# The router computed with one batch per partition, and the first tile's second half normalised and rounded behind the choice of experts

## The chip, the cores and the metric

One core of a Trainium2 chip. The metric is the device time of one execution in microseconds (us). TensorE (PE in the profile, PEld its weight loads) does the matmuls, VectorE is DVE, ScalarE is ACT, GpSimd is POOL, SyncE (SP) issues most of the transfers. Each engine runs its own queue in order; where one needs another's result, its instruction waits for a semaphore. SBUF is the memory on the chip, PSUM the banks that TensorE writes.

## The reference, cut to what matters

x is (8, 64, 32, 32): 8 batches, 64 channels, 1024 tokens. First comes a channel attention block with a residual, then a mixture of experts whose router sees only the mean token of a batch, so each batch has one choice of two experts out of eight:

```python
x = x + _L0_conv_ref(_ln_c(x), Wqkv, bqkv, Wout, bout, 8)
t = _to_tokens(x)
t = t + _L0_ffn_ref(_ln_t(t), Wr, br, W1, b1, W2, b2, gamma, beta)
# in _L0_ffn_ref, x being _ln_t(t):
logits = jnp.mean(x, axis=1) @ Wr + br                       # (8 batches, 8 experts)
routing_weights = jax.nn.softmax(logits, axis=-1)
expected_loads = routing_weights.sum(axis=0) * (N / B)
scale = jnp.where(expected_loads > capacity, capacity / expected_loads, 1.0)
routing_weights = jax.nn.softmax(routing_weights * scale, axis=-1)
top_w, top_i = jax.lax.top_k(rw_tok, K)                      # K = 2
top_w = jax.nn.softmax(top_w, axis=-1)
h = jax.nn.gelu(jnp.einsum('nd,edf->enf', xf, W1) + b1[:, None, :], approximate=False)
y = jnp.einsum('enf,efd->end', h, W2) + b2[:, None, :]
out = _layer_norm(out + x, gamma, beta)                      # out: the two chosen y, weighted
```

The kernel computes only the two chosen experts of each batch.

## The kernel before, in words

The data lie with channels on the partitions, two batches to a tile of 128 partitions: four tiles p = 0 to 3, each with 1024 columns. After the attention block `T` holds the residual stream, 128 x 1024 per tile; columns 0 to 511 of a tile are its batch half b = 0, 512 to 1023 its half b = 1. The queues of all engines are written out by hand, and nothing reorders them.

Around the change this happens. `scores(p)` multiplies T by the router's weights on TensorE, `evac_scores` copies the result to SBUF, `turn_scores` transposes it into `ps_sc`. `turned_stats` and `rstd2` give `r2`, one over the deviation of every token (semaphore `pow2`). `weigh_scores` and `sum_scores` (DVE) weigh the scores with r2 and sum them; `logits` sums over the partitions with a matrix of ones, which leaves all 64 logits on each of the 128 partitions. From there DVE and ACT work through softmax, loads, scale, `largest` (the eight largest values of a batch, `m8`) and `indices` (their places, `i8`). The semaphore `top` tells that indices are there, batches 0 and 1 first. The second softmax and the weights of the two experts are worked out with two Tanh on ACT; `wk` holds the weights.

Meanwhile the tile's values are normalised: `spread2(p, b)` spreads r2 over the channels with matmuls into the PSUM bank `rb[p][b]`, `normal2(p, b)` (DVE) multiplies T by it into `UF` (semaphores s_uf0 to s_uf7), `round_hi` (ACT) rounds that to fp16 in `HI`, and `low` (POOL) puts the rest in `LO`. For p = 1 and 3 spread2 works with bf16 rows in `RR` (made by split3 on POOL, turn2 on PE and a copy on ACT); for p = 0 and 2 with fp32 matmuls from r2 itself. `centre_w1` and `centre_w2` centre the experts' weights; `split_w1` (ACT) and `low_w1` (POOL) split W1 into two fp16 parts in `w1hl`; `w2c` is centred W2.

Once the experts are known, `gather_w1` copies the weights of one batch's expert into `w1g` and `gather_w2` those of W2 times `wk` into `w2g`. The expert layers are steps: `up(step, i)` is the first matmul of an expert for one batch (six matmuls of 512 columns: HI with both weight parts, LO with one), `gelu(step, i)` on ACT, and `down(step, i)` the second matmul into `y_ps` (bank pC). `residual3(p, ...)` puts the centred input into y_ps ahead of the down matmuls, from `ST`, a copy of HI and LO that SP's transfers make. y_ps and the two halves of rb[2] are the same bank, so residual3(0, (0,)) waits until normal2(2, 0) has read rb[2][0] (s_uf4), and residual3(0, (1,)) until normal2(2, 1) has (s_uf5).

PE's queue runs on as up(0,0), up(0,1), up(1,0), residual3(0,(0,)), down(0,0), up(1,1), residual3(0,(1,)), down(0,1), down(1,0), down(1,1), up(2,0). Gelu needs another table of functions on ACT than Exp, so the kernel calls a one-column Gelu (`gtab`) ahead of the first real one.

Of the kernel before, what the change touches and what calls it, by code (L numbers as in the profile page):

```python
# [8 lines left out]
BF16 = mybir.dt.bfloat16  # L9
# [43 lines left out]
def build_program(nc, x_tok, x_cha, small, w12, consts, constb, out):  # L53
# [11 lines left out]
    with ExitStack() as ctx:  # L65
# [23 lines left out]
        w1f = SQ[:, 0, :]  # L89
# [40 lines left out]
        brz = sb("brz", [P, B * E])  # L130
        ssw = sb("ssw", [P, B * E])
        ones_m = sb("ones_m", [P, P])
        rout = sb("rout", [P, 4, B * E])
        rx = sb("rx", [P, 2, (E + 1) * B])
        rsm = sb("rsm", [P, 8, B])
        m8 = sb("m8", [P, B, 8])
        i8 = sb("i8", [P, B, 8], U32)
        wk = sb("wk", [P, B, TOP])
# [3 lines left out]
        i8f = sb("i8f", [P, TOP, B])  # L142
        hot = sb("hot", [P, TOP, B * E])
# [49 lines left out]
        rb = [[pB[:, HALF:N], pA[:, HALF:N]], [pS[:, :], pM[:, :]], [pC[:, 0:HALF], pC[:, HALF:N]], [pS[:, :], pM[:, :]]]  # L193
# [4 lines left out]
        def pair_view(ap):  # L198
# [19 lines left out]
        ps_lg = pM[:, 0:B * E]  # L218
        px = [pB[:, i * B * E:(i + 1) * B * E] for i in range(3)]
# [46 lines left out]
        def _(sp):  # L266
# [12 lines left out]
            for b in range(2):  # L279
                cols = slice(b * HALF, (b + 1) * HALF)  # L280
                for half, src, done in ((0, HI, s["hi"]), (1, LO, s["lo"])):
                    sp.wait_ge(done, b + 1)
                    for h in range(2):
                        sp.dma_start(ST[half * C:(half + 1) * C, b, h * HALF:(h + 1) * HALF],
                                     src[h * C:(h + 1) * C, 0, cols]).then_inc(s_st[b], 16)
            for p in range(1, NP):
                for half, src, done in ((0, HI, s["hi"]), (1, LO, s["lo"])):
                    if (p, half) == (NP - 1, 0):
                        sp.wait_ge(s["hi3"], 2)
                    else:  # L290
                        sp.wait_ge(done, 2 * p + 2 - half)
# [24 lines left out]
        def _(act):  # L316
# [32 lines left out]
            def split_w1(h):  # L349
# [4 lines left out]
                nc.scalar.mul(w1hl[:, e, 0, :], src, S_W).then_inc(s["w1h"], 1)  # L354
                nc.scalar.mul(w1f[:, h * HALF:(h + 1) * HALF], ps_w1[h], S_W).then_inc(s["w1f"], 1)
# [80 lines left out]
            act.wait_ge(s["top"], 1)  # L436
            first = {(0, 0): nc.scalar.value_load(i8[0:1, 0, 0:1], min_val=0, max_val=E - 1)}
            act.wait_ge(s["w1h"], 2)
            act.wait_ge(s["w1l"], 2)
            nc.scalar.copy(w1g[:, 0, 0, 0, :, :], w1hl[:, bass.ds(first[0, 0], 1), :, :]).then_inc(s["w1g_first"], 1)  # L440
            act.wait_ge(s["rx2"], 1)
            nc.scalar.activation(rx[:, 1, :], rx[:, 0, :], ACT.Tanh, scale=0.5).then_inc(s["rexp2"], 1)

            def half_tanh():
                act.wait_ge(s["rx3"], 1)
                nc.scalar.activation(rsm[:, 7, :], rsm[:, 6, :], ACT.Tanh, scale=0.5).then_inc(s["half_tanh"], 1)
# [56 lines left out]
            half_tanh()  # L503
# [39 lines left out]
        def _(pool):  # L543
# [36 lines left out]
            def load_experts(p):  # L580
                pool.wait_ge(s["top"], min(p + 1, 3))
                experts = [[load_expert(p, k, b) for b in range(2)] for k in range(TOP)]
# [26 lines left out]
            nc.gpsimd.memset(ones_m[:, :], 1.0 / (S_U * N)).then_inc(s["onesm"], 1)  # L609
# [4 lines left out]
            for h in range(2):  # L614
# [15 lines left out]
            split3(nc.gpsimd, link, 0, 2, r2[:, 1:NP:2, :], s["s2"])  # L630
            low_w1(0)
            low_w1(1)
            low(0, 0)
            low(0, 1)
            pool.wait_ge(s["top"], 1)
            pool.wait_ge(s["w1h"], 2)
            pool.wait_ge(s["w1l"], 2)
            pool.wait_ge(s["w2v"], 2)
            experts = [[0, 0], [0, 0]]
            for k, b in ((0, 1), (1, 0), (1, 1)):  # L640
                experts[k][b] = load_expert(0, k, b)
                gather_w1(0, k, b, experts[k][b])
            experts[0][0] = load_expert(0, 0, 0)
# [28 lines left out]
        def _(dve):  # L672
# [107 lines left out]
            def weigh_scores(g):  # L780

                dve.wait_ge(s["sc"], 2 * g + 2)
                dve.wait_ge(s["pow2"], 1)
                src = ps_sc[g][:, 0:4 * P].rearrange("p (j r) -> p j r", r=32)[:, :, 0:2 * E]
                link(nc.vector.tensor_tensor(
                    sw[:, 2 * g * P:2 * (g + 1) * P].rearrange("p (j h e) -> p j h e", h=2, e=E),
                    src.rearrange("p j (h e) -> p j h e", h=2),
                    r2[:, 2 * g:2 * g + 2, :].rearrange("p n (j h) -> p (n j) h", h=2).unsqueeze(3)
                    .broadcast_to([P, 2 * CH, 2, E]), ALU.mult))
# [736 lines left out]
```

## Time and profile before

| what | us |
|---|---|
| runs shown: median, lowest, highest of 3 | 94.47, 94.15, 95.64 |
| the profiled execution | 94.27 |
| its span, first to last instruction | 92.4 |
| PE busy | 81.0 (88%) |
| DVE busy | 62.1 |
| ACT busy | 51.0 |
| POOL busy | 38.7 |

The span is 1.87 us shorter than the time of the same execution; that rest lies around the span. The mean granted TensorE clock over the span is 0.991 of full speed. Rows of the profile give a start and a duration in us, the engine, the line of the kernel, the operation, what it writes and reads, and in brackets how long its engine was idle before it and what released it.

### The profile page before, as it was taken

The numbers are of one execution on the slowest core, as the hardware profiler recorded it, in microseconds if no ns is written. First come the engines' busy times: TensorE is split into PE (matmuls) and PEld (weight loads), VectorE is DVE, ScalarE is ACT, GpSimd is POOL, SyncE is SP. The second block draws the span as 40 slices with busy tenths as digits, with TensorE's granted clock in tenths as the row PEclk, the third lists the DMA queues.
The fourth block names the chain that finished last, engine by engine and source line by source line (L and its number), as shares of the span: only waits on it lengthen the run. The fifth ranks groups of instructions, "written<-read, shape, count | busy, mean of one in ns | idle before, by whom it ended". The sixth has DMA issues, their size and how long they took to land.

```text
span 92.4 us, 2203 instructions
## 1 busy us (share of the span) xinstructions
PE 81.0 (88%) x723; PEld 42.8 (46%) x723; DVE 62.1 (67%) x225; ACT 51.0 (55%) x91; POOL 38.7 (42%) x90
## 2 busy tenths in 40 slices
PE   4995999999799999997769996999989999998900
PEld 1343699899654356486623341323324332344500
DVE  0089998981749798899899869741555374649560
ACT  0050505416388533379759989967995879644000
POOL 6000090000000050299334499947960850499900
PEclk9999999999999999999999999999999999999996
DMA  2899999991000000001430033880050036008573
GB/s 42 260 401 321 296 269 249 264 257 30 0 7 0 0 0 0 11 0 30 112 86 4 7 83 75 198 200 16 0 121 0 0 86 141 0 19 200 141 202 127
DMA packets 6715, 9.82 MB, mean 106 GB/s; under 512 B 1073, under 2 KB 3633, under 8 KB 6705
## 3 DMA queue, kind: packets, MB, share of 16 engines
q1 hardware_dynamic: 5408, 7.56, 32.1%
q10 hardware_dynamic: 1296, 2.13, 7.6%
q8 instruction: 6, 0.10, 0.4%
q14 instruction: 5, 0.03, 0.1%
HBM read 5.49 MB, written 2.10 MB: 82 GB/s over the span
## 4 chain that ended last, share of the span: by engine, by line
PE 52%; DVE 12%; ACT 12%; DMA 8%; POOL 7%; issue 4%; ACTq 2%; DVEq 0%; POOLq 0%
PE pC L1351 10%; DMA cst<-consts_dram 8%; PE pA L1327 5%; ACT H L480 5%; PE pB L1033 4%; PE pS L1033 4%; PE pA L1043 4%; POOL r L603 4%; PE pB L1327 3%; POOL XT L252 3%; PE pC L1095 2%; PE pS L1095 2%; PE pC L1343 2%; PE pA L1110 2%; DVE bst L762 2%
## 5 line engine op out<-in xcount | busy, mean ns | idle before, releaser
L1351 PE MATMUL pC<-H,w2g 128*64 128x512 f32 x64 | 15.9, 603 | 0.0
L705 DVE BATCH_NORM_STATS2 bst<-XT 128x6 f32<-128x128 f32 x32 | 6.5, 286 | 5.0 <-DMA XT<-x_tok_dram 5.0
L627 POOL TENSOR_TENSOR T<-UF,X 128x512 f32<-128x512 f32 x1 | 1.3, 1270 | 19.0 <-ACT UF L417 19.0
L1246 PE MATMUL pM<-wz 128*128 128x512 bf16 x25 | 7.7, 473 | 1.3 <-POOL wz L552 1.3
L480 ACT ACTIVATE H<-pA,b1s 128x1024 f32<-128x1024 f32 x6 | 6.7, 1115 | 2.8 <-PE pA L1327 2.7
L562 POOL TENSOR_TENSOR LO<-UF,HI 128x512 f16<-128x512 f32 x7 | 8.0, 1158 | 0.0
L578 POOL COPY w1g<-w1hl 128x256 f16 x15 | 5.9, 425 | 3.8 <-issue 2.5
L480 ACT ACTIVATE H<-pB,b1s 128x1024 f32<-128x1024 f32 x6 | 6.7, 1123 | 0.1
L242 POOL CAST R<-r 128x16 bf16<-128x16 f32 (+1 forms) x4 | 0.8, 201 | 14.2 <-DVE r L696 14.2
L1327 PE MATMUL pA<-HI,w1g 64*128 64x512 f16 x32 | 4.9, 380 | 2.1 <-ACT H L480 1.5
L252 POOL TENSOR_TENSOR XT<-XT,T 128x512 f32<-128x512 f32 x5 | 6.3, 1271 | 0.0
L1351 PEld LDWEIGHTS pC<-H,w2g 128*64 128x64 f32 x64 | 4.0, 136 | 5.0 <-issue 4.1
L332 ACT COPY U<-pA 128x1024 f32<-128x1024 f32 x4 | 4.0, 1012 | 3.8 <-PE pA L1043 3.7
L259 POOL TENSOR_TENSOR UT<-XT,rt 128x512 f32<-128x512 f32 x2 | 2.0, 1045 | 9.1 <-DVE UT L259 9.1
L949 DVE TENSOR_SCALAR U<-pC,c,wsm 128x512 f32<-128x512 f32 x6 | 4.7, 800 | 1.2 <-PE pC L1351 0.9
L594 POOL TENSOR_TENSOR w2g<-w2c,wk 128x64 f32<-128x64 f32 x16 | 4.7, 319 | 1.6 <-DVE wk L894 1.4
L1246 PEld LDWEIGHTS pM<-wz 128*128 128x128 bf16 x25 | 2.7, 117 | 5.3 <-issue 2.7
L1327 PE MATMUL pB<-HI,w1g 64*128 64x512 f16 x32 | 4.9, 378 | 0.0
L382 ACT ACTIVATE T<-T,wsm 128x1024 f32<-128x1024 f32 x4 | 4.6, 1158 | 0.0
L493 ACT ACTIVATE SQ<-pC,c 128x512 f32<-128x512 f32 x6 | 4.0, 688 | 1.1 <-DVE U L949 0.6
L968 DVE COPY RR<-pS 48x128 bf16<-48x128 bf16 x3 | 0.6, 216 | 5.8 <-PE pS L1163 5.8
L385 ACT ACT_TABLE_LOAD x1 | 1.3, 1283 | 5.6 <-issue 5.6
(247 smaller groups left out, 196.4 us busy)
## 6 DMA issues: line engine op xcount, KB each, us to landing
X<-x_cha_dram SPq DMA_DIRECT2D x16, 128.0 KB, 10.1
out_dram<-XT SPq DMA_DIRECT2D x11, 128.0 KB, 2.4
XT<-x_tok_dram SPq DMA_DIRECT2D x2, 512.0 KB, 9.2
ST<-HI SPq DMA_DIRECT2D x6, 128.0 KB, 2.4
ST<-LO SPq DMA_DIRECT2D x6, 128.0 KB, 2.4
XT<-x_tok_dram SPq DMA_DIRECT2D x2, 256.0 KB, 4.7
XT<-x_tok_dram ACTq DMA_DIRECT2D x2, 256.0 KB, 4.9
w_sb<-w_dram ACTq DMA_DIRECT2D x4, 128.0 KB, 8.9
```

The costliest lines, as they stand in the source:

```text
L252: engine.tensor_tensor(OUT[:, p, cols], V[:, p, cols], T[:, p, cols], ALU.add).then_inc(s_fin[2 * p + h], 1)
L382: nc.scalar.activation(T[:, p, :], T[:, p, :], ACT.Identity, bias=w("beta")).then_inc(s["tbeta"], 1)
L480: nc.scalar.activation(H[:, step % 2, i, :], h_ps[i][:, :], ACT.Gelu, bias=bias, scale=1.0 / (S_U * S_W)).then_inc(s["gelu"], 1)
L562: nc.gpsimd.tensor_tensor(LO[:, p, cols], UF[:, p, cols], HI[:, p, cols], ALU.subtract).then_inc(s["lo"], 1)
L578: nc.gpsimd.tensor_copy(w1g[:, p % 2, k, b, :, :], w1hl[:, bass.ds(expert, 1), :, :]).then_inc(s["w1g"], 1)
L594: nc.gpsimd.tensor_tensor(w2g[:, p % 2, b, k, :], w2c[:, bass.ds(experts[k][b] * C, C)], wk[:, 2 * p + b, k:k + 1].broadcast_to([P, C]), A ...
L705: return nc.vector.bn_stats(bst[:, p, j, :], XT[:, p, j * P:(j + 1) * P].rearrange("p (b c) -> p c b", b=2))
L949: nc.vector.tensor_scalar(ZS[:, p, cols], y_ps[:, cols], c2[:, i:i + 1], w("gamma"), ALU.add, ALU.mult).then_inc(s["zs"], 1)
L1033: last = mm(ps_g[g][:, l * G1:(l + 1) * G1], UT[:, p, j, 1:P + 1], UT[:, p, j, :], start=(j == 0), stop=(j == CH - 1))
L1246: mm(pM[:, :], wz[:, 0:P], wz[:, :], start=True, stop=True)
L1327: last = mm(h_ps[i][:, h * HALF:(h + 1) * HALF], w1g[h * C:(h + 1) * C, p % 2, k, b, a, :], src[h * C:(h + 1) * C, p, b * HALF:(b + 1) * H ...
L1351: last = mm(half(y_ps[:, b * HALF:(b + 1) * HALF], h), w2g[:, p % 2, b, k, :], H[:, step % 2, i, h * HALF:(h + 1) * HALF], start=False, st ...
```

## The change: what it does

The router is computed with one batch on each of eight partitions. The raw scores are copied to SBUF (`copy_scores`, ACT), `sum_scores` on TensorE multiplies them by r2 and sums over the tokens (eight matmuls of 8 rows and 64 columns), and two small DVE operations and one matmul (`logits`) give an 8 x 8 tile of logits. Exp on ACT gives the sums as well (accum_out). `loads` is a matmul over the eight partitions. One MAX and one MAX_INDEX serve all batches, so `top` comes once. The second softmax uses Exp instead of Tanh (`ex2`, `e01`, `eu`), and one matmul (`choice`) brings weights and indices from 8 partitions to all 128 (`ps_bc`, copied to `wk`).

Of the first tile, normal2(0, 1) now stands behind MAX_INDEX on DVE, and round_hi(0, 1) behind the wait for `top` on ACT; LO of that half is made on DVE (semaphore `lo01`) instead of POOL. The copies of `w2c` move from ACT to DVE, half of LO of W1 moves from POOL to DVE, and the first expert's gather from ACT to POOL. spread2(2, *) works with RR rows instead of fp32; spread2(1, *) moves behind up(0, 1). normal2 runs in the order (1,0), (2,0), (1,1), (2,1).

```diff
         def normal2(p, b):
                 i = 2 * p + b
-                dve.wait_ge(s["rb"], i + 1)
+                dve.wait_ge(s["rb"], 2 * (0, 2, 1, 3)[p] + b + 1)
...
-            weigh_scores(0)
-            weigh_scores(1)
-            for g in range(2):
-                last = sum_scores(g)
-            last.then_inc(s["ssw"], 1)
+            dve.wait_ge(s["w1h"], 1)
+            nc.vector.tensor_tensor(w1hl[:, 0:E // 2, 1, :], ps_w1[0].rearrange("p (e f) -> p e f", f=F),
+                                    w1hl[:, 0:E // 2, 0, :], ALU.subtract).then_inc(s["w1l0"], 1)
+            dve.wait_ge(s["lq"], 1)
...
             normal2(0, 0)
+            dve.wait_ge(s["lg"], 1)
+            nc.vector.tensor_reduce(nlm[:, :], ps_lg, AX_X, ALU.max, negate=True).then_inc(s["nlm"], 1)
+            dve.wait_ge(s["rexp1"], 1)
+            nc.vector.reciprocal(ri[:, :], es[:, :]).then_inc(s["ri"], 1)
+            dve.wait_ge(s["load"], 1)
...
+            nc.vector.max(m8[:, :], rout[:, :]).then_inc(s["m8"], 1)
+            dve.wait_ge(s["m8"], 1)
+            nc.vector.max_index(i8[:, :], m8[:, :], rout[:, :]).then_inc(s["top"], 1)
+            normal2(0, 1)
+            dve.wait_ge(s["rexp2"], 2)
...
+            for h in range(2):
+                nc.vector.tensor_copy(w2c[:, h * HALF // 2:(h + 1) * HALF // 2], ps_w2[h]).then_inc(s["w2v"], 1)
...
+            dve.wait_ge(s["hi"], 2)
+            nc.vector.tensor_tensor(LO[:, 0, HALF:N], UF[:, 0, HALF:N], HI[:, 0, HALF:N],
+                                    ALU.subtract).then_inc(s["lo01"], 1)
+            dve.wait_ge(s["bc"], 1)
+            nc.vector.tensor_copy(wk[:, :, :], ps_bc.rearrange("p (b k) -> p b k", b=B)).then_inc(s["wkd"], 1)
+            normal2(1, 0)
+            normal2(2, 0)
+            normal2(1, 1)
+            normal2(2, 1)
...
             round_hi(0, 0)
-            act.wait_ge(s["rx1"], 1)
-            nc.scalar.activation(px[0], rout[:, 1, :], ACT.Exp).then_inc(s["rexp1"], 1)
             act.wait_ge(s["rt2"], 1)
-            nc.scalar.copy(RR[:, :, :], ps_rt2.rearrange("p (k n) -> p k n", k=2)).then_inc(s["rr2"], 1)
+            nc.scalar.copy(RR[:, :, :], ps_rt2.rearrange("p (k n) -> p k n", k=3)).then_inc(s["rr2"], 1)
+            act.wait_ge(s["rout"], 1)
+            nc.scalar.activation(ex2[:, :], rout[:, :], ACT.Exp, accum_out=es2[:, :]).then_inc(s["rexp2"], 1)
...
+            act.wait_ge(s["top"], 1)
             round_hi(0, 1)
-            act.wait_ge(s["w2p"], 1)
-            for h in range(2):
-                nc.scalar.copy(w2c[:, h * HALF // 2:(h + 1) * HALF // 2], ps_w2[h]).then_inc(s["w2v"], 1)
...
+            act.wait_ge(s["de"], 1)
+            nc.scalar.activation(eu[:, :], de[:, :], ACT.Exp, scale=ri2[:, :]).then_inc(s["rexp3"], 1)
             nc.scalar.activation(gtab[:, :], w("bout"), ACT.Gelu)
...
+            centre_w1()
             turn_scores(2)
             turn_scores(3)
-            centre_w1()
-            bias_logits()
+            sum_scores()
             spread2(0, 0)
+            logits()
             spread2(0, 1)
-            logits()
             turn2()
+            loads()
             for i in range(2):
                 centre_w2(i)
             for b in range(2):
-                spread2(1, b)
-            for b in range(2):
                 spread2(2, b)
...
+            up(0, 0)
+            choice()
+            up(0, 1)
             for b in range(2):
-                up(0, b)
+                spread2(1, b)
             up(1, 0)
```

On PE, from the spreading for the third tile (rb[2], bank pC) to the second step's first up, before:

```order
L1201 MATMUL pC<-cst,r2 64x128 [waits s_w2v,s_pow2]
L1201 MATMUL pC<-cst,r2 64x128 x7
L1201 MATMUL pC<-cst,r2 64x128 [waits s_w2v,s_pow2]
L1201 MATMUL pC<-cst,r2 64x128 x7
L1327 MATMUL pA<-HI,w1g 128x512 [waits s_w1g_first,s_hi,s_w1l,s_w1h]
L1327 MATMUL pA<-HI,w1g 128x512 x3
L1327 MATMUL pA<-LO,w1g 128x512 [waits s_lo]
L1327 MATMUL pA<-LO,w1g 128x512
L1327 MATMUL pB<-HI,w1g 128x512 [waits s_hi,s_w1g]
L1327 MATMUL pB<-HI,w1g 128x512 x3
```

and now (L1153 is spread2 from RR, L1214 `choice`, L1326 `up`):

```order
L1153 MATMUL pC<-RR,cstb 128x128 [waits s_w2v,s_rr2,s_pow2]
L1153 MATMUL pC<-RR,cstb 128x128 x3
L1153 MATMUL pC<-RR,cstb 128x128 [waits s_w2v,s_rr2,s_pow2]
L1153 MATMUL pC<-RR,cstb 128x128 x3
L1326 MATMUL pA<-HI,w1g 128x512 [waits s_hi,s_w1g,s_w1f]
L1326 MATMUL pA<-HI,w1g 128x512 x3
L1326 MATMUL pA<-LO,w1g 128x512 [waits s_lo]
L1326 MATMUL pA<-LO,w1g 128x512
L1214 MATMUL pM<-mk,ones 128x32 [waits s_mk,s_ones8]
L1326 MATMUL pB<-HI,w1g 128x512 [waits s_hi,s_w1g]
L1326 MATMUL pB<-HI,w1g 128x512 x3
L1326 MATMUL pB<-LO,w1g 128x512 [waits s_lo01]
```

The sixteen fp32 matmuls for the third tile have become eight bf16 ones that wait for RR too, choice stands between the first two ups with a wait for mk, and the second up takes its LO half behind lo01. Behind that second up:

```order
L1326 MATMUL pB<-LO,w1g 128x512
L1153 MATMUL pS<-RR,cstb 128x128 [waits s_bc,s_rr2,s_pow2]
L1153 MATMUL pS<-RR,cstb 128x128 x3
L1153 MATMUL pM<-RR,cstb 128x128 [waits s_wkd,s_rr2,s_pow2]
L1153 MATMUL pM<-RR,cstb 128x128 x3
L1326 MATMUL pA<-HI,w1g 128x512 [waits s_gelu,s_w1g]
L1326 MATMUL pA<-HI,w1g 128x512 x3
L1326 MATMUL pA<-LO,w1g 128x512 x2
L1342 MATMUL pC<-ST,cstb 64x512 [waits s_st0,s_uf4]
```

The spreading for the second tile (pS, pM) has moved here, its first half behind bc and its second behind wkd, ahead of the second step's up and of residual3 (L1342), which waits for s_uf4.

On DVE, from the largest values to the weights, before:

```order
L863 MAX m8<-rout 128x8 [waits s_dve]
L863 MAX m8<-rout 128x8 x3
L866 MAX_INDEX i8<-m8,rout 128x8 [waits s_dve]
L866 MAX_INDEX i8<-m8,rout 128x8
L863 MAX m8<-rout 128x8 x4
L876 TENSOR_TENSOR rx<-m8 128x8 [waits s_dve]
L877 TENSOR_TENSOR rx<-rout,m8 128x64
L800 TENSOR_TENSOR UF<-T,pC 128x512 [waits s_rb]
L883 TENSOR_SCALAR rx<-rx 128x72 [waits s_rexp2]
L884 RECIPROCAL rx<-rx 128x72 [waits s_dve]
L885 TENSOR_REDUCE rsm<-rx 128x8 [waits s_dve]
L886 TENSOR_SCALAR rsm<-rsm 128x8 [waits s_dve]
```

and now, to the copy of wk and the first two normal2 behind it (left out are four small operations on 8 partitions, of which the first after the wait for eu is dn):

```order
L799 TENSOR_TENSOR UF<-T,pB 128x512 [waits s_rb]
L859 RECIPROCAL ri2<-es2 8x1 [waits s_rexp2]
L860 TENSOR_TENSOR de<-e01 8x1
L863 COPY w2c<-pC 128x256 [waits s_w2p]
L863 COPY w2c<-pC 128x256
...
L870 TENSOR_TENSOR mk<-val,s8 8x32 [waits s_dve]
L873 TENSOR_TENSOR LO<-UF,HI 128x512 [waits s_hi]
L876 COPY wk<-pM 128x32 [waits s_bc]
L799 TENSOR_TENSOR UF<-T,pS 128x512 [waits s_rb]
L799 TENSOR_TENSOR UF<-T,pC 128x512 [waits s_rb]
```

The half of the first tile (UF<-T,pB), the w2c copies and LO have come between the choice and the third tile's normal2 (UF<-T,pC), which before stood directly behind the MAX instructions.

On ACT, from the Exp of the router to the first Gelu, before:

```order
L427 ACTIVATE pB<-rout 128x64 [waits s_rx1]
L429 COPY RR<-pA 48x256 [waits s_rt2]
L378 CAST HI<-UF 128x512 [waits s_uf1]
L433 COPY w2c<-pC 128x256 [waits s_w2p]
L433 COPY w2c<-pC 128x256
L435 ACT_TABLE_LOAD
L435 ACTIVATE gtab<-wsm 128x1
L437 TENSOR_LOAD i8 [waits s_top]
L437 ISA x2
L440 ISA [waits s_w1l,s_w1h]
L440 COPY w1g<-w1hl 128x256
L442 ACTIVATE rx<-rx 128x72 [waits s_rx2]
```

and now:

```order
L455 ACTIVATE ex2,es2<-rout 8x8 [waits s_rout]
L457 ACTIVATE e01<-m8 8x2 [waits s_m8]
L399 CAST HI<-UF 128x512 [waits s_uf1,s_top]
L460 TENSOR_LOAD i8
L460 ISA x2
L462 ACTIVATE eu<-de,ri2 8x1 [waits s_de]
L463 ACT_TABLE_LOAD
L463 ACTIVATE gtab<-wsm 128x1
L497 ISA [waits s_mm1]
L497 ACTIVATE H<-pA,wsm 128x1024
```

The second rounding has moved behind `top`, and the table load behind it and behind the Exp that makes eu; the copies of w2c and the first gather have left ACT.

## Rows read from the trace of the kernel before

**Rows 1.** The chain that ended last, 38 to 52 us: start, duration, what.

```profile
38.39 0.24 DVE r L696
...
39.64 1.15 DVE ssw L792 x2
...
43.61 1.28 ACT L435
...
45.63 0.41 ACT w1g L440
...
46.34 0.84 PE pA L1327 x6
...
47.30 1.12 ACT H L480
...
48.56 0.82 PE pA L1327 x6
...
49.39 0.34 PE pC L1343 x2
...
51.34 0.34 PE pC L1343 x2
```

**Rows 2.** PE in order of time: start, duration, line, operation.

```profile
37.51 0.69 PE L1227 MATMUL pC<-w_sb,cst 64*128 64x512 f32 x1
...
38.93 1.09 PE L1201 MATMUL pB<-cst,r 128*64 128x128 f32 x16
...
40.84 0.43 PE L1213 MATMUL pM<-ssw,ones_m 128*128 128x64 f32 x2
...
42.56 0.38 PE L1168 MATMUL pS<-RR,cstb 48*128 48x128 bf16 x4
...
42.79 0.38 PE L1168 MATMUL pM<-RR,cstb 48*128 48x128 bf16 x4
```

**Rows 3.** ACT in order of time, 20 to 45 us.

```profile
20.47 0.35 ACT L337 ACTIVATE Ex<-sm,nmx 128x64 f32<-128x64 f32 x1 [2.96 <-DVE nmx L736]
...
20.72 0.19 ACT L337 ACTIVATION_READ_ACCUMULATOR Ex<-sm,nmx 128x1 f32 x1
...
38.67 0.60 ACT L354 ACTIVATE w1hl<-pC 128x512 f16<-128x512 f32 x1 [1.58 <-PE pA L1227]
...
42.43 0.62 ACT L378 CAST HI<-UF 128x512 f16<-128x512 f32 x1
...
42.95 0.64 ACT L433 COPY w2c<-pC 128x256 f32<-128x256 f32 x2
...
44.90 0.20 ACT L435 ACTIVATE gtab<-wsm 128x1 f32<-128x1 f32 x1
```

**Rows 4.** ACT line that reads the expert number, from its queue.

```profile
L437 ACTq TENSOR_LOAD <-i x1: 480/480/480, 44.7 to 44.7; - x1
```

**Rows 5.** DVE in order of time, 38 to 54 us.

```profile
38.72 0.42 DVE L785 TENSOR_TENSOR sw<-pS,r 128x256 f32<-128x256 f32 x1
...
41.72 0.68 DVE L800 TENSOR_TENSOR UF<-T,pA 128x512 f32<-128x512 f32 x1
...
43.33 0.21 DVE L858 RECIPROCAL pB<-rsm 128x8 f32<-128x8 f32 x1
...
44.52 0.16 DVE L866 FIND_INDEX8 i<-m,rout 128x8 uint32<-128x8 f32 x1
...
53.28 0.22 DVE L928 TENSOR_REDUCE c<-hb 128x8 f32<-128x64 f32 x1
```

**Rows 6.** POOL in order of time.

```profile
42.11 2.27 POOL L562 TENSOR_TENSOR LO<-UF,HI 128x512 f16<-128x512 f32 x2
...
45.63 0.40 POOL L578 COPY w1g<-w1hl 128x256 f16 x1 [1.25 <-DVE i L866]
```

**Rows 7.** DMA issues by line: KB each, us from issue to landing.

```profile
ST<-LO SPq DMA_DIRECT2D x4, 64.0 KB, 2.1
```

**Rows 8.** Stretch after the last matmul: busy of PE, PEld, DVE, ACT, POOL; then PEclk.

```profile
87.90:90.50 2.60, 0.00 (x0) 0.00 (x0) 1.25 (x4) 0.00 (x0) 0.04 (x1) 1.00 0.75 213
```

More of the change, by code:

```diff
@@ L129, in build_program @@
         SR = sb("SR", [P, 2, 2 * P])
[L130 to L138, printed above, removed]
+        cendS = sb("cendS", [P, P])
+        ones = sb("ones", [B, P])
+        s8 = sb("s8", [P, B])
+        lm = sb("lm", [P, B + 1, E])
+        ls = sb("ls", [P, E])
+        nlm = sb("nlm", [B, 1])
+        ex = sb("ex", [B, E])
+        es = sb("es", [B, 1])
+        ri = sb("ri", [B, 1])
+        fe = sb("fe", [B, 2, E])
+        rout = sb("rout", [B, E])
+        ex2 = sb("ex2", [B, E])
+        es2 = sb("es2", [B, 1])
+        ri2 = sb("ri2", [B, 1])
+        m8 = sb("m8", [B, 8])
+        i8 = sb("i8", [B, 8], U32)
+        e01 = sb("e01", [B, TOP])
+        de = sb("de", [B, 1])
+        eu = sb("eu", [B, 1])
+        dn = sb("dn", [B, 1])
+        val = sb("val", [B, 2 * TOP])
+        mk = sb("mk", [B, B, 2 * TOP])
+        wk = sb("wk", [P, B, 2 * TOP])
         w1g = sb("w1g", [P, 2, TOP, 2, 2, F], F16)
@@ L280, in _ @@
                 cols = slice(b * HALF, (b + 1) * HALF)
-                for half, src, done in ((0, HI, s["hi"]), (1, LO, s["lo"])):
-                    sp.wait_ge(done, b + 1)
+                for half, src, done in ((0, HI, s["hi"]), (1, LO, s["lo"] if b == 0 else s["lo01"])):
+                    sp.wait_ge(done, 1 if half else b + 1)
                     for h in range(2):
@@ L290, in _ @@
                     else:
-                        sp.wait_ge(done, 2 * p + 2 - half)
+                        sp.wait_ge(done, 2 * p if half else 2 * p + 2)
                     if half:
@@ L437, in _ @@
[L437 to L446, printed above, removed]
@@ L502, in _ @@
             gelu(0, 0)
-            half_tanh()
             gelu(0, 1)
@@ L580, in load_experts @@
             def load_experts(p):
[L581 to L582 removed]
+                experts = [[0, 0] for k in range(TOP)]
+                if p:
+                    experts = [[load_expert(p, k, b) for b in range(2)] for k in range(TOP)]
                 for k in range(TOP):
                     for b in range(2):
+                        if p == 0:
+                            experts[k][b] = load_expert(p, k, b)
                         gather_w1(p, k, b, experts[k][b])
@@ L894, in _ @@
-            nc.vector.tensor_scalar(wk[:, :, 1], rsm[:, 7, :], 0.5, 0.5, ALU.mult, ALU.add).then_inc(s["wkd"], 1)
-            indices(2)
-            indices(3).then_inc(s["top"], 1)
-            for b in range(2):
-                normal2(1, b)
-            for i in range(4, B):
-                last = indices(i)
-            last.then_inc(s["top"], 1)
-            dve.wait_ge(s["top"], 3)
             dve.wait_ge(s["iota"], E)
+            dve.wait_ge(s["wkd"], 1)
+            dve.wait_ge(s_uf[2], 1)
@@ L1174, in turn2 @@
                 pe.wait_ge(s["s2"], 1)
-                pe.wait_ge(s["w1f"], 2)
-                for i in range(2):
+                pe.wait_ge(s["scs"], 2)
+                for i in range(NP - 1):
                     last = turn(ps_rt2[:, i * P:(i + 1) * P], i)
@@ L1324, in up @@
                     elif k == 0 and n != 1:
-                        pe.wait_ge(done, 2 * p + b + 1 - (n == 2 and p >= 2))
+                        pe.wait_ge(done, 2 * p + b + 1 - ((p >= 1) + (p >= 2) if n == 2 else 0))
                     for h in range(2):
```

226 lines of the change are left out of this document (107 added, 119 removed).

## The prediction

> **What bounds the kernel now.** I read the chain that ended last first, because the change lies in one short stretch and only what it does to that chain counts. From the last step of r2 on DVE at 38.39 the chain runs through the summing of the scores, then through ACT (rounding, copies of w2c, the load of the Gelu table at 43.61), the first expert's gather at 45.63, the first up at 46.34, the first Gelu at 47.30, and from 48.56 on it stays on PE: up, residual3 at 49.39, down, up, residual3 at 51.34 [rows 1]. In the order of time I then read PE, ACT, DVE and POOL of that stretch for the durations [rows 2, 3, 5, 6]. The reader is to see two marks: the first Gelu starts at 47.30, and residual3(0,(0,)) at 49.39. Behind that PE has no gap in the chain until after 51.34, so the end moves by as much as residual3 moves, unless something later is late. I found nothing later that becomes earlier or later by itself: all ups, Gelus and downs stay.
>
> **The change: the router, up to `top`.** r2 is there at 38.39 + 0.24 = 38.63, as before [rows 1]. What follows it changes.
> - The centring of W1 moves ahead of the last two turned scores. It started at 37.51 and ACT took its result at 38.67 [rows 2, 3]. The two blocks change places, so the pair ends where it ended, at 38.65 at the latest; as the transposes then wait for ACT no longer, I take 38.4. The turned scores thus come 0.9 later than the 37.5 of before, nearly hidden by the r2 chain, which needs until 38.63.
> - ACT copies the second half of the scores (128 x 256, some 0.4 us, by the DVE row of that size at 0.42 [rows 5] and the 0.64 of two ACT copies of it [rows 3]): 38.85. Eight matmuls of 64 columns give lq. The trace has none with 8 rows; it lies between 0.43, a single fp32 product of 64 columns, and 1.09, eight of 128 columns [rows 2]. I take 0.55, nearer to the first since four of them write different strips of rows: 39.45.
> - In exchange the two weighing and two summing steps go, which ran from 38.72 to 39.64 + 1.15 = 40.79 [rows 1, 5]. Two small DVE steps at about 0.22 follow; ls is there at 39.95. The new subtraction of W1 on DVE (38.7 to 39.4, by the 0.68 of a 512-column row [rows 5]) lies under the wait for lq.
> - PE spreads the first half (1.09 [rows 2]) from 39.4 to 40.45, DVE normalises it until 41.15, logits is done by then, and the maximum at 41.35.
> - Exp with its sum: an Exp of 64 columns and the reading of its sum end 0.44 after the start (20.47 to 20.72 + 0.19 [rows 3]); here 41.8. Reciprocal (0.21 [rows 5]) 42.05. The matmul `loads` at 0.43 [rows 2] 42.5. Three small steps, MAX and MAX_INDEX at 0.2 to 0.25 each: `top` at 43.65.
>
> Before, `top` was at 44.52 + 0.16 = 44.68 [rows 5]. So the choice comes 1.0 us earlier. The uncertain terms are lq (0.43 to 1.09, that is -0.1 to +0.5) and seven handovers between engines, which I took at 0.05 (summing ends at 40.79, PE's next weight-carrying matmul starts at 40.84 [rows 1, 2]) and which could cost 0.1 more each: +0.7.
>
> **What eats this gain.** Before, DVE had the half normal2(0,1) behind it at 41.72, beside the Exp [rows 5]. Now it stands behind `top`:
> - DVE: normal2(0,1) 43.7 to 44.35; ri2 and de to 44.7; the two w2c copies, 0.64 on ACT [rows 3] and up to twice 0.42 on DVE [rows 5], I take 0.75: 45.45.
> - PE: spread2(2,*) waits for w2v, because its bank is that of w2c, and it stands ahead of up(0,0). It is now eight bf16 matmuls, which the other tile's took from 42.53 to 42.79 + 0.38 = 43.17, 0.64 [rows 2]: 45.5 to 46.1. So PE waits for w2v, while POOL has the first gather ready: it came 0.95 after `top` and takes 0.40 [rows 5, 6], thus by 45.05. up(0,0) at 0.84 [rows 1] ends at 46.95.
> - ACT: rounding of that half (0.62 [rows 3]) 44.4 to 45.0; the expert number is read meanwhile (0.48 [rows 4]); eu to 45.3; the table load at 1.28 [rows 1] to 46.6; gtab at 0.20 [rows 3] to 46.8. The first Gelu then waits for PE only, and starts at 47.05. It gains 0.25 against 47.30, not 1.0. The cover over the table load is thin: 0.15.
> - The weights: mk on DVE from eu by four small steps to 46.3, LO of the half to 47.0, PE takes choice at 46.95, up(0,1) to 47.9 and spread2(1,0) to 48.2 (half of the 0.64). wk is copied at 47.3, and POOL's first gather of W2 is in time for the down.
> - DVE: normal2(1,0) 48.25 to 48.95, normal2(2,0) to 49.65, each 0.68 [rows 5]. Only then may residual3(0,(0,)) write its bank: 49.7 against 49.39 [rows 1]. Before, that half was normalised directly behind MAX and nobody waited for it. up(1,0), from 48.4 to 49.25, is no longer the last thing that residual3 waits for.
>
> **The sum:** residual3 moves by 49.7 - 49.39 = +0.3 us. Behind it, residual3(0,(1,)) waits for normal2(2,1), at 49.65 + 2 x 0.68 = 51.05, and for the transfer of LO, whose issue is at 47.1 plus a second one of about 1.2 and 2.1 to land [rows 7], near 50.4; both are ahead of 51.34 + 0.3. The biases' block on DVE ended at 53.28 + 0.22 [rows 5]; it starts 0.2 later than before and ends near 53.7, still ahead of the second tile's evacuation. On POOL, low of the half (half of 2.27 [rows 6]) is gone and gathers are earlier, which frees about 1 us that no one waits for. The profiled execution took 94.27, so I predict 94.27 + 0.3 = 94.6, which is 0.1 over the median of the runs shown, 94.47.
>
> The Trainium skill ("ScalarE: Activation LUTs", section "What ACT_TABLE_LOAD costs") adds a drain of about 1.38 us to the 1.28 of a table load for every change of set. Here the load starts right behind the w2c copies and gtab follows it at 44.90, 1.29 after 43.61 [rows 1, 3], so the trace shows no drain there. By the page the first Gelu would come 1.38 later than I reckon by way of the table.
>
> **The rivals.**
> - *Faster: the waits for w2v and s_uf4 are shorter.* If lq and the w2c copies take their lower ends and PE hands over faster, 0.3 + 0.1 + 0.1 go, and with shorter small steps (8 partitions instead of 128) some 0.3 more. Then residual3 could come at 48.9, but up(1,0) bounds it: Gelu at 46.9 at the earliest gives up(1,0) to 49.0. Gain 0.4: 93.9. For it speaks that the choice is 1 us earlier; against it, that a DVE step of 8 columns costs 0.16 to 0.21 [rows 5] by its start alone.
> - *Slower: the longer hand-to-hand chain.* The router now crosses between engines some ten times up to the weights. With lq at 1.09 and the handovers 0.1 us dearer, everything behind the r2 step is 1.1 later, and since residual3 is at the end of that same chain, nothing absorbs it: 94.6 + 0.9 = 95.5. It decides for slower than before from the point at which `top` comes after 43.35, by the sum above.
> - *The table load is not hidden.* It now stands behind an Exp of eight rows instead of a copy; if that made it cost its row once more, 1.28 [rows 1], the first Gelu would be at 48.1, up(1,0) would run from 49.3 to 50.2 instead of ending at 49.39, and the time would be 94.27 + 0.8 = 95.1. That gtab followed the load at once [rows 3] speaks against it. The page named above would make it much the same.
> - *The clock.* PE has nothing from the centring of W2 (about 43.4) to 45.5, a pause of 2.1 us. The only pause of that length that the trace shows is after the last matmul: in 2.6 us the granted clock stayed at 1.00 (2.4 GHz) [rows 8]. If it fell to 1.2 GHz all the same, the next ups would take twice 0.84 each, and two of them give +1.7: 96.3.
>
> **How the numbers follow.** Forecast 94.6 with chance 0.5; faster rival 93.9 with 0.2; longer chain 95.5 with 0.2; table 0.05; clock 0.05. The range holds 0.8: it leaves out the clock and the outer halves of the two large rivals, 93.6 to 95.7. A measurement of this kernel can tell about 2%, 1.9 us; no case but the clock's comes near that. Chances: faster 0.05, same 0.86, slower 0.09.
>
> **What would show it.** In the trace of the changed kernel: MAX_INDEX ending near 43.65; the w2c copies on DVE near 45.45 and spread2(2,*) right behind them; the table load from 45.3 to 46.6; the first Gelu near 47.05; residual3 held by UF<-T,pC of DVE and starting near 49.7; the granted clock at 1.00 throughout. The prediction is wrong in its core if residual3 is held by up(1,0) or the Gelu instead, or if a step before 38.6 moves.

## The result and the profile after

The changed kernel is slower: 97.78 us in the median of 5 executions (96.83 to 98.13) against 94.48 (94.15 to 95.64), a ratio of 1.0323 with a 95% interval of 1.0272 to 1.0374. The profiled execution took 96.83 with a span of 94.5; before, it was 94.27 with 92.4. So 2.1 of its 2.56 us lie in the span and 0.46 outside it. Outside the span lay 1.87 in the profiled execution of before, 1.8 to 2.2 in its other executions and 2.3 in all five of the changed kernel; that part stays unexplained.

The first look is at the clock, since the forecast stood on a full one. The view of stretches of the changed kernel (start and end; length; busy time of PE, PEld, DVE, ACT, POOL, each with its number of instructions; then the granted clock):

```profile
43.20:45.60 2.40, 0.01 (x1) 0.00 (x0) 2.27 (x11) 1.03 (x5) 0.58 (x2) 1.00 0.43 107
45.60:47.40 1.80, 1.65 (x18) 1.11 (x20) 1.39 (x5) 1.77 (x4) 0.92 (x3) 1.00 0.25 63
47.40:50.60 3.20, 3.20 (x20) 1.56 (x20) 1.69 (x5) 2.11 (x2) 1.43 (x6) 0.51 0.21 51
50.60:52.00 1.40, 1.40 (x9) 0.40 (x10) 1.37 (x6) 1.07 (x2) 1.36 (x4) 0.90 0.00 0
```

PE has nothing to do for 2.4 us, works again from 45.6, and at 47.4 the clock falls from 2.4 to 1.2 GHz and stays there for 3.4 us, until 50.8, through nothing but matmuls. The other four executions have only a mean clock, and it is lower still: 0.949 to 0.954, against 0.968 in the profiled one and 0.991 in the profiled one of before. (A mean also holds the end of the program, where the clock falls in every kept trace although PE has no more work, and where that costs nothing.) So the profiled execution, the fastest of the five, is the mildest case. As an estimate from the means, if the end was as in the profiled one (2.7 us at half clock), the others ran 6 to 7 us of matmuls at 1.2 GHz, as experiments 2 and 10 show it in a trace.

The chain of the changed kernel, where it answers to [rows 1]:

```profile
42.12 0.21 DVE fe L849
...
42.35 1.07 DVE fe L850
...
43.89 0.23 DVE i L856 x2
44.11 0.58 DVE UF L799
...
44.83 0.68 DVE w2c L863 x2
...
45.64 0.49 PE pC L1153 x6
...
47.01 0.37 PE pM L1214 x2
47.38 1.28 PE pB L1326 x6
48.66 0.42 PE pS L1153 x4
49.08 0.21 PE pM L1153 x2
...
49.51 1.28 PE pA L1326 x5
50.79 0.40 PE pC L1342 x2
```

Up to 47.38 the reader can lay this beside the forecast's own times: w2c copied at 45.5 (forecast 45.45), spread2(2,*) from 45.6, choice at 47.0 (46.95). From there each up takes 1.28 us instead of the 0.82 to 0.84 of [rows 1], and residual3 comes at 50.79 instead of 49.39, right behind up(1,0). One step stands out before that: L850, an operation on 8 x 8 elements, took 1.07 us. Beside it ran this on POOL (order of time, changed kernel):

```profile
42.24 1.15 POOL L578 TENSOR_TENSOR LO<-UF,HI 128x512 f16<-128x512 f32 x1 [1.05 <-ACT HI L399]
```

POOL's subtraction ended at 43.39, the small step at 43.41. The same happens once more behind the first layer (order of time, changed kernel, POOL and DVE):

```profile
55.15 2.27 POOL L578 TENSOR_TENSOR LO<-UF,HI 128x512 f16<-128x512 f32 x2 [0.36 <-ACT HI L399]
...
56.56 1.41 DVE L920 TENSOR_TENSOR LO<-UF,HI 128x512 f16<-128x512 f32 x1
```

A step of this shape takes 0.67 alone. PE's first moment rows, at 57.93 before, are at 60.03 here: the 1.4 us from residual3 have become 2.1, which is the whole difference of the spans.

### The profile page after: what moved, and what is told of

Its sections match the earlier page's. It is cut to its first block, busy times and chain, and to the rows that moved or that the text cites. A ratio compares the mean times of both kernels' runs of the same rounds, so it can differ in the third digit from the quotient of the medians.

```text
span 94.5 us, 2174 instructions
## 1 busy us (share of the span) xinstructions
PE 81.5 (86%) x718; PEld 42.7 (45%) x718; DVE 60.5 (64%) x200; ACT 51.1 (54%) x93; POOL 37.7 (40%) x93
## 4 chain that ended last, share of the span: by engine, by line
PE 56%; DVE 14%; DMA 8%; POOL 7%; ACT 7%; issue 3%; ACTq 1%; DVEq 0%; POOLq 0%
PE pC L1350 10%; DMA cst<-consts_dram 8%; PE pB L1018 4%; PE pA L1028 4%; PE pA L1326 4%; PE pS L1018 4%; POOL r L620 4%; PE pB L1326 4%; ACT H L497 3%; DVE UF L799 3%; POOL XT L264 3%; DVE U L936 2%; PE pA L1095 2%; PE pC L1080 2%; PE pC L1342 2%
## 5 line engine op out<-in xcount | busy, mean ns | idle before, releaser
L1248 PE MATMUL pM<-wz 128*128 128x512 bf16 x25 | 8.3, 503 | 1.3 <-POOL wz L568 1.3
L578 POOL TENSOR_TENSOR LO<-UF,HI 128x512 f16<-128x512 f32 x6 | 6.9, 1158 | 2.1 <-ACT HI L399 2.1
L1326 PE MATMUL pA<-HI,w1g 64*128 64x512 f16 x32 | 5.8, 411 | 0.1
L1326 PE MATMUL pB<-HI,w1g 64*128 64x512 f16 x32 | 5.3, 401 | 0.0
```

The costliest lines, as they stand in the source:

```text
L578: nc.gpsimd.tensor_tensor(LO[:, p, cols], UF[:, p, cols], HI[:, p, cols], ALU.subtract).then_inc(s["lo"], 1)
L1248: mm(pM[:, :], wz[:, 0:P], wz[:, :], start=True, stop=True)
L1326: last = mm(h_ps[i][:, h * HALF:(h + 1) * HALF], w1g[h * C:(h + 1) * C, p % 2, k, b, a, :], src[h * C:(h + 1) * C, p, b * HALF:(b + 1) * H ...
```

## The experiments

Each kernel ran beside the kernel before on the same chip; a ratio is its executions against those of before, with a 95% interval. All but the last are edits of the changed kernel. The added matmuls feed nothing, and no kernel leaves out part of the computation. Experiments 1 to 4 ran on one chip, 5 to 8 on a second, 9 to 11 on a third and 12 on the first again; between them kernels are compared by their ratios.

**1. PE kept busy in the pause.**

```diff
             for i in range(2):
                 centre_w2(i)
+            keep_awake(10)
```

> The changed kernel with ten more bf16 matmuls of 512 columns (their result is read by nobody) behind the centring of W2, in PE's pause from 43.2 to 45.6. Theory A, the clock: the pause made the granted clock fall to 0.50 from 47.4 to 50.6, and that costs about 1 us; with PE kept busy the clock stays at 1.00, residual3 starts near 49.9 instead of 50.72, and the time falls from 97.8 to about 96.5. Rival B, waits alone: DVE and ACT set the stretch and PE would wait as long at full clock; the clock stays at 1.00 and the time stays within 0.3 us of 97.8.

Measured: 95.45 us (95.27 to 95.91), ratio 1.0079 (1.0042 to 1.0115). The stretches of its profiled execution:

```profile
43.00:45.30 2.30, 2.11 (x9) 0.80 (x9) 2.14 (x11) 1.06 (x5) 0.46 (x2) 1.00 0.46 114
45.30:47.00 1.70, 1.58 (x18) 1.03 (x20) 1.32 (x5) 1.67 (x4) 0.86 (x3) 1.00 0.22 55
47.00:50.60 3.60, 3.23 (x29) 1.36 (x28) 2.82 (x8) 3.50 (x5) 1.83 (x7) 1.00 0.22 54
```

The clock stays at 1.00, and 2.3 us are back (the ratio falls from 1.032 to 1.008). Theory A had the direction and underrated the size, since it was read from the mildest execution; rival B falls. In the order of time residual3 now stands where before had it (49.32), and the bracket says who holds it:

```profile
49.40 0.41 PE L1347 MATMUL pC<-ST,cstb 128*64 128x512 f16 x2 [0.37 <-DVE UF L799]
```

**2. The loads' reciprocal in PSUM, and 3. both.**

```diff
-            link(nc.vector.reciprocal(fe[:, 0, :], ps_load))
-            link(nc.vector.tensor_scalar(fe[:, 1, :], fe[:, 0, :], CAPACITY / N, 1.0, ALU.mult, ALU.min))
+            link(nc.vector.reciprocal(ps_load, ps_load))
+            link(nc.vector.tensor_scalar(fe[:, 1, :], ps_load, CAPACITY / N, 1.0, ALU.mult, ALU.min))
```

> The changed kernel with the reciprocal of the loads left in PSUM, so that the 8 x 8 TENSOR_SCALAR behind it reads PSUM instead of SBUF. Theory A: that step took 1.06 us because it ended only when POOL's subtraction for LO ended; reading PSUM it takes 0.2, top comes 0.85 earlier, PE's pause shrinks from 2.4 to 1.6 us, the clock may stay at 1.00, and the time falls to about 96.0 to 97.0. Rival B: the operation is slow by itself on 8 partitions; it stays at about 1 us and the time does not change.

> Both edits: the loads' reciprocal in PSUM and eight matmuls in the pause. If the clock and the held step are the two causes and add up, the first Gelu is near 46.9 (bound by the table load), residual3 near 49.0 to 49.4, and the time is 94.5 to 95.5, what is left over coming from DVE's subtraction for LO of the second tile, which took 1.41 us instead of 0.77. If the rest of the chain is what costs, it stays above 96.

Measured: alone 97.57, 98.2 and 97.49 us at a mean clock of 0.949 to 0.957, and 95.94 at 0.969; with eight matmuls in the pause 95.22 (95.04 to 95.37), ratio 1.0036 (1.0002 to 1.0070). DVE in order of time, reciprocal in PSUM alone:

```profile
42.14 0.15 DVE L850 TENSOR_SCALAR fe<-pM 8x8 f32<-8x8 f32 x1
42.33 0.86 DVE L851 SCALAR_TENSOR_TENSOR rout<-ex,ri,fe 8x8 f32<-8x8 f32 x1
```

The step that now reads PSUM takes 0.15, so it was not slow by itself. But the next one, with two inputs in SBUF, took its place: 0.86 instead of 0.21, again until POOL's subtraction ended (42.01 + 1.16 = 43.17). Of the expected 0.85 us only 0.2 came (MAX_INDEX ends 5.08 behind the end of r2 instead of 5.27). Half of theory A holds; the size I expected does not. PE's pause was still 2.2 us, and in this execution the clock fell inside it, at 44.9, and stayed at 0.50 until 51.7. With both edits the time is in the expected range.

**4. The second half ahead of the choice again.**

```diff
             nc.vector.reciprocal(ri[:, :], es[:, :]).then_inc(s["ri"], 1)
+            normal2(0, 1)
...
             nc.vector.max_index(i8[:, :], m8[:, :], rout[:, :]).then_inc(s["top"], 1)
-            normal2(0, 1)
...
+            round_hi(0, 1)
             act.wait_ge(s["rout"], 1)
...
             act.wait_ge(s["top"], 1)
-            round_hi(0, 1)
```

> The kernel with the loads' reciprocal in PSUM, and the first tile's second half normalised on DVE behind ri, ahead of the loads, and rounded on ACT ahead of the second Exp: the part of the change that put both behind the choice is undone. If that place costs, top comes 0.3 to 0.6 later but the w2c copies 0.2 to 0.4 earlier and PE's pause is shorter; the time is 0.2 to 0.5 below that of the kernel with the reciprocal in PSUM alone. If the place is right, it is 0 to 0.5 above.

Measured on top of the edit of 2: 95.7, 96.33, 97.27 and 97.31 us, at a mean clock of 0.982, 0.976, 0.951 and 0.952. The clock covers the question, so this run decides nothing; experiment 9 repeats it. PE's pause was 1.7 us in its trace, and the clock fell at 46.1, until 49.5.

**5. POOL kept away from DVE's subtraction; 6. the router without two SBUF inputs; 7. the third tile's half first; 8. all of it.** 5 and 7 have ten matmuls in the pause, 6 and 8 six. 8 holds the edits of 5, 6 and 7 together.

```diff
# 5
+            pool.wait_ge(s["lo11"], 1)
             low(2, 0)
             low(2, 1)
# 6
-            link(nc.vector.reciprocal(fe[:, 0, :], ps_load))
-            link(nc.vector.tensor_scalar(fe[:, 1, :], fe[:, 0, :], CAPACITY / N, 1.0, ALU.mult, ALU.min))
-            nc.vector.scalar_tensor_tensor(out=rout[:, :], in0=ex[:, :], scalar=ri[:, :], in1=fe[:, 1, :],
+            link(nc.vector.reciprocal(ps_load, ps_load))
+            link(nc.vector.tensor_scalar(ps_load, ps_load, CAPACITY / N, 1.0, ALU.mult, ALU.min))
+            nc.vector.scalar_tensor_tensor(out=rout[:, :], in0=ex[:, :], scalar=ri[:, :], in1=ps_load,
# 7
-            normal2(1, 0)
             normal2(2, 0)
+            normal2(1, 0)
             normal2(1, 1)
```

> The changed kernel with ten matmuls in PE's pause (as in the first experiment, 95.45 us), and GpSimd's subtraction for LO of the third tile made to wait until DVE's subtraction for LO of the second tile is done. Theory A, collision: DVE's subtraction took 1.33 to 1.41 us instead of 0.77 because GpSimd's, now earlier, ran beside it; kept apart it takes 0.77, the second tile's second evacuation and the next ups come 0.6 earlier, and the time falls by 0.5 to 0.6, to about 94.9. Rival B: the operation is slow for another reason, or GpSimd's delay is passed on; the time stays at 95.4 or rises.

> The changed kernel with six matmuls in PE's pause, and the loads' reciprocal, its clipping and the last product of the router all reading the loads from PSUM, so that none of them has two inputs in SBUF. With the reciprocal alone in PSUM the wait only moved to the product with two SBUF inputs (0.87 us, ending with GpSimd's subtraction). Theory A: now no step is held, top comes at about 42.85 instead of 43.66, the first Gelu at 46.2, residual3 at 48.6, and the time falls from 95.2 to 94.5. Rival B: the product is held whatever its inputs; no change. Rival C: top comes earlier, but the table load or the gathers on GpSimd take over, and the time falls by less than 0.3.

> The changed kernel with ten matmuls in PE's pause and the third tile's first half normalised ahead of the second tile's (it is spread already, and DVE waits 0.78 us there for the spreading of the second). If residual3 is held by that half, as forecast, it starts at 49.0 (behind the up of the second step) instead of 49.40, and the time falls by 0.3 to 0.4 to 95.1. If not, no change.

> All of it: six matmuls in the pause, the router's loads in PSUM, GpSimd waiting for DVE, the third tile's half first. If the causes add up: 97.8 less 2.3 (clock) less 0.8 (held router step) less 0.6 (held subtraction) less 0.4 (order), 93.7 to 94.0, which is 0.5 to 1 us below the kernel before. If the table load ahead of the first Gelu bounds it, 94.2 to 94.5.

| kernel | us, median (range) | ratio to before (95%) |
|---|---|---|
| 1: matmuls in the pause | 95.45 (95.27 to 95.91) | 1.0079 (1.0042 to 1.0115) |
| 5: and POOL waits | 94.81 (94.54 to 95.22) | 1.0007 (0.9962 to 1.0053) |
| 6: and the router in PSUM | 94.69 (94.49 to 96.42) | 0.9997 (0.9956 to 1.0037) |
| 7: and the third tile's half first | 94.49 (94.14 to 96.57) | 0.9969 (0.9918 to 1.0020) |
| 8: all of them | 93.57 (93.23 to 95.37) | 0.9859 (0.9752 to 0.9965) |

By the ratios, 5, 6 and 7 are 0.7, 0.8 and 1.1% under 1, each to about 0.6%; the traces say where.

5: DVE's subtraction takes 0.68 instead of 1.41 and POOL starts behind it; theory A holds in place and size (0.6 us). DVE and POOL in order of time:

```profile
55.44 0.68 DVE L921 TENSOR_TENSOR LO<-UF,HI 128x512 f16<-128x512 f32 x1
```

```profile
56.20 2.28 POOL L578 TENSOR_TENSOR LO<-UF,HI 128x512 f16<-128x512 f32 x2 [2.18 <-DVE LO L921]
```

6: no router step is held. From the end of r2 to the end of MAX_INDEX it takes 44.82 - 40.44 = 4.4 us, against 43.79 - 38.45 = 5.3 in experiment 1; the time falls by 0.8, as theory A had it. The product itself:

```profile
44.15 0.21 DVE L851 SCALAR_TENSOR_TENSOR rout<-ex,ri,pM 8x8 f32<-8x8 f32 x1
```

POOL's subtraction ran beside it (43.83 to 44.99). MAX8 and FIND_INDEX8, which read SBUF, took 0.16 and 0.15 beside it as well, so not every small step with its inputs in SBUF is held.

In the profiled executions of 6 and 8 the clock fell early in the program, from 10.8 to 14.3, so that only differences from the end of r2 are read; they are the 96.42 and the 95.37 of the table. PE had waited there for a transfer for 2.1 and 2.3 us, behind some 5 us of dense matmuls of 512 columns, in a stretch that the change does not touch (stretches of number 8):

```profile
5.00:7.10 2.10, 2.10 (x10) 0.77 (x8) 2.10 (x12) 1.28 (x1) 0.00 (x0) 1.00 1.06 405
7.10:9.40 2.30, 0.01 (x1) 0.01 (x1) 2.09 (x12) 0.00 (x0) 0.00 (x0) 1.00 1.05 323
...
10.80:14.30 3.50, 3.50 (x16) 2.85 (x14) 3.50 (x17) 0.86 (x8) 2.82 (x5) 0.51 1.05 279
```

7: residual3 starts 10.5 us behind the end of r2 (49.12 - 38.61) instead of 10.95 (49.40 - 38.45) in experiment 1. So the half of the third tile did hold it, by the 0.4 that was expected. The time fell by 1.0, more than expected: DVE's subtraction met POOL's at another moment, and this time POOL's pair was the one that got longer, 2.72 instead of 2.27, while DVE's took 0.69:

```profile
53.89 2.72 POOL L578 TENSOR_TENSOR LO<-UF,HI 128x512 f16<-128x512 f32 x2
```

8: the parts add up, apart from the collision, which 5 and 7 both remove: 93.57 where the sum gave 93.7 to 94.0, less than the kernel before by 1.4%.

**9, 10 and 11.** Number 8 with the edit of 4; number 8 without the matmuls in the pause; number 8 once more.

> The kernel with all four edits (matmuls in the pause, loads in PSUM, GpSimd waiting, third tile's half first; 93.57 us), and the first tile's second half again ahead of the choice: normalised behind ri on DVE, rounded ahead of the second Exp on ACT. This undoes the part that the change is named after, with the clock and the collisions out of the way. If the place behind the choice costs, DVE's 0.68 us leaves the way to the w2c copies while the router waits there for the loads for only 0.3, so the step to spread2(2) gets 0.3 us shorter and the time falls by 0.2 to 0.3. If the table load ahead of the first Gelu binds, it changes by less than 0.1. If the place was right, it rises by 0.2 to 0.4.

> The kernel with all edits but the matmuls in PE's pause; the router is 1 us shorter, so the pause is 1.5 us instead of 2.4. Theory A: a pause of 1.5 us is still one in which the clock falls in some or all executions; the time is 94.5 to 96 and scattered. Rival: the shorter pause leaves the clock alone, and the time is 93.5 as with the matmuls.

> The kernel with all four edits once more, beside the two others on the same chip, for a closer comparison with the kernel before: 93.4 to 93.8, ratio 0.985 to 0.992.

| kernel | us, every execution | mean clock |
|---|---|---|
| 9 | 92.94 to 93.47, median 93.09 | 0.984 to 1.000 |
| 10 | 93.32 | 1.000 |
| 10 | 96.11, 96.25, 96.27, 96.40, 97.14 | 0.953 to 0.959 |
| 11 | 93.38 to 93.66, median 93.50 | 0.989 to 1.000 |

The ratios to before are 0.9821 (0.9777 to 0.9864) for 9 and 0.9858 (0.9817 to 0.9900) for 11. Number 10 is the cleanest look at the clock: one and the same program, 93.32 us where it did not fall and about 3 us more where it did. The stretches of its profiled execution:

```profile
43.10:44.60 1.50, 0.00 (x0) 0.01 (x1) 1.45 (x6) 0.65 (x2) 0.57 (x2) 1.00 0.39 98
44.60:45.60 1.00, 0.97 (x13) 0.78 (x14) 0.60 (x4) 0.98 (x2) 0.59 (x2) 0.83 0.47 115
45.60:52.00 6.40, 6.40 (x32) 2.64 (x28) 4.73 (x15) 4.42 (x6) 3.33 (x10) 0.50 0.18 45
```

Here a pause of 1.5 us was followed, 0.7 us after PE had resumed, by 6.8 us at 1.2 GHz (45.3 to 52.1). Number 9 answers the question of number 4: with clock and collisions out of the way, the place behind the choice costs 0.4 us (93.50 to 93.09; what of it is DVE's half and what ACT's rounding, which moved together, is not separated). In number 9 the whole stretch starts 0.23 earlier (r2 ends at 38.71 against 38.94); counted from there the choice itself comes 0.18 later (MAX_INDEX ends 4.61 behind it, against 4.43), so of the 0.68 us of normal2(0,1) only that much falls on the choice, and the rest where DVE waits for others anyway. Behind the choice the order turns round: the w2c copies start at 43.47 against 44.02, which is 0.32 earlier counted from r2, and the table load 0.48 earlier:

```profile
44.45 1.28 ACT L463 ACT_TABLE_LOAD   x1
```

It is at 45.16 in number 11. Residual3 starts 9.25 us behind the end of r2 (47.96 - 38.71) against 9.61 (48.55 - 38.94), which is the 0.4 in its place.

**12. The kernel before, its own pauses filled.**

```diff
+            pe.wait_ge(s_uf[0], 1)
+            for _ in range(3):
+                mm(pB[:, HALF:N], cb("identb"), cb("sel")[:, 0:HALF], start=True, stop=True)
             for b in range(2):
                 spread2(2, b)
+            for _ in range(2):
+                mm(pB[:, HALF:N], cb("identb"), cb("sel")[:, 0:HALF], start=True, stop=True)
```

> The kernel before with five more matmuls of 512 bf16 columns whose result nobody reads: three ahead of the spreading for the third tile and two behind it, where PE paused for 0.7 and 0.6 us. A quarter of the executions of the kernel before had a mean clock of 0.972 to 0.975 and took 95.0 to 95.6 instead of 94.4 to 94.9. If a falling clock behind these pauses does that, the filled kernel has none of them: its highest time is under 95 and its median 0.1 to 0.2 lower. If the scatter comes from elsewhere in the program, it keeps executions at 0.973.

Measured: 94.38 us (93.94 to 94.92, 12 executions), ratio 0.9966 (0.9937 to 0.9996). None has a clock under 0.986. Of the 17 executions of before beside it, four are at 0.972 to 0.975, and they took 95.15 to 95.80. This fits pauses in this stretch as the cause of the scatter of the kernel before: in all experiments together 20 of its 72 executions are at 0.972 to 0.975, and none of the 12 filled ones. It is not shown, since no trace of such an execution was kept, and experiments 6 and 8 show a fall in another stretch, which the five matmuls leave as it is.

## Why the prediction was wrong

It gave 94.6 in 93.6 to 95.7 and 0.09 for slower by over 2%; the time is 97.78.

- **The step that failed is the clock: the sum let it stay at 1.00 throughout and left its fall to the rival "The clock".** The rival named the right pause (2.1 us, measured 2.4), put 0.05 on it and priced it at +1.7. I took [rows 8], a pause of 2.6 us at full clock, as a bound for all pauses. That stretch ended just before the fall: in the same pause of the kernel before the clock fell at 90.6, 2.8 us after the last matmul.

```profile
90.50:92.40 1.90, 0.00 (x0) 0.00 (x0) 0.00 (x0) 0.00 (x0) 0.00 (x0) 0.54 0.29 90
```

  In the fourteen kept traces the clock falls 1.9 (changed kernel) to 5.0 us (experiment 4) after the last matmul, so a single reading there bounds nothing. What PE did before the pause does not part the cases either: the pauses of 2.1 and 2.3 us in experiments 6 and 8 stand behind dense matmuls and were followed by a fall, and in experiment 10 the same program with a pause of 1.5 us fell in five executions and not in the sixth. What decides in which execution it falls stays open. The price was short too: experiment 1 gives 2.3, and 10 gives 2.8 to 3.8, since not two ups but all matmuls of 3.4 to 6.8 us run at half speed, and they are the chain. The Trainium skill ("TensorE: Matmul & The Clock Gate", section "What's actually happening") says that the gate on TensorE's clock is set by how busy PE has been recently. The traces agree in that the fall need not come in the pause: it came 1.8 us after PE had taken up work again in the changed kernel, 0.7 us in experiment 10, and inside the pause in experiment 2.
- **"Three small steps, MAX and MAX_INDEX at 0.2 to 0.25 each: top at 43.65."** It came at 44.11, 0.2 of that because r2 was later in this execution (it ended at 38.84). One step took 1.07 because POOL's subtraction ran beside it. The reciprocal I took the duration from (0.21 [rows 5]) writes PSUM, and the kernel before had placed just this value there; its MAX_INDEX at 44.52 ran after POOL's subtractions had ended. Experiments 2 and 6 show that for the step and the product behind it the place of the inputs decides: worth 0.8 us. The Trainium skill ("GPSIMD Engine Reference", section "1. Specifications") says of GpSimd's SBUF interfaces: "Shared with VectorE (contention with DVE instructions in a 2-port perf mode or with two SBUF inputs)". The runs agree for two SBUF inputs: 0.86 and 1.41 instead of 0.21 and 0.68. The step of 1.07 has one tensor input, and whether it ran in such a mode no trace shows.
- **"Frees about 1 us that no one waits for", on POOL.** The earlier POOL ran into DVE's subtraction of the second tile, which delayed PE by 0.6 (experiment 5). The freed time was harmful, by a term that the sum did not have.
- **Held residual3.** Not so in the changed kernel: it follows up(1,0), which at half clock ended at 50.79, while normal2(2,0) had ended at 50.40. The forecast named this as the sign that its core is wrong. With the clock repaired the reading holds: residual3 waits for the half of the third tile, by 0.4 (experiments 1 and 7). Its place is then 49.40, where I had 49.7, although `top` was late; the handovers took 0.02 to 0.05, most of them less than I allowed, and the eight-row matmuls 0.42 instead of 0.55.
- **The table load.** Right in its cost: 1.28 and gtab right behind it (45.90, 47.19 in the changed kernel). The cover of 0.15 was not there: the first up had ended at 46.89, and the first Gelu came behind gtab at 47.30, not at 47.05. With the clock repaired residual3 waited for DVE all the same (experiment 1).
- **That the late half costs.** I charged it with most of the lost gain. It costs 0.4 (experiment 9). It also lengthens PE's pause, 2.2 us in experiment 2 against 1.7 in 4, but the clock fell in the traces of both, so that this helped the fall is not shown.

In sum, of the 3.05 us that the ratio of 1.0323 makes: the clock 2.3; with the clock repaired 0.75 remain, and the held router step (0.8) and the collision behind the first layer (0.6) more than account for them. With the clock kept up, the holds removed, the third tile's half first and the late half back ahead of the choice, the kernel takes 93.1 us, 1.8% under the kernel before. How much of that is the router with one batch per partition is not shown: number 9 keeps the other moves of the change and six added matmuls, and five such matmuls alone gave the kernel before 0.3% (experiment 12).

## What to carry to other kernels

When a change shortens work on TensorE in a stretch where others compute something small, look at its pause, and at the clock of every execution and not of the profiled one alone; one pause that passed at full clock says nothing about the next, and a stretch that is to serve as evidence must be read to its end; a few matmuls without use can be the cheapest repair. Before moving a DVE step or making POOL faster, list what POOL runs at that moment, and keep one input of short DVE steps in PSUM. A cause with a small chance and a large price deserves its own row of evidence from a like stretch, or a wider range.

## What the runs showed of the hardware

- After a pause of TensorE of 2.4 us (changed kernel) or 1.5 us (number 10) the granted clock fell from 1.00 to 0.50, 1.8 and 0.7 us after work had begun again, and stayed there for 3.4 and 6.8 us; in experiment 2 it fell inside the pause. Behind dense matmuls it did the same: after pauses of 2.1 and 2.3 us (experiments 6 and 8, the fall at 10.8) and, at the end of the program, 1.9 to 5.0 us after the last matmul.
- The same program falls or does not: number 10 did in five of six executions.
- A DVE step of 8 x 8 elements took 1.07 (one SBUF input, SBUF output) or 0.86 us (two SBUF inputs) beside a GpSimd subtraction, and 0.15 to 0.21 with its second or only tensor input in PSUM. MAX8 and FIND_INDEX8 from SBUF took 0.16 and 0.15 beside one (number 6).
- Two subtractions of the same form on DVE and GpSimd hold each other either way: DVE's took 1.41 instead of 0.68 (changed kernel), or GpSimd's pair 2.72 instead of 2.27 (number 7).
